# Query copies in halves within the first pass, and maxima rows of twelve heads within the second pass, in a cross-attention layer

## What is computed

```python
q = _split_heads(query_modal @ Wq.T + bq)          # 512 queries, 16 heads of 32
k = _split_heads(key_value_modal @ Wk.T + bk)      # 8192 keys
v = _split_heads(key_value_modal @ Wv.T + bv)
scores = jnp.einsum('bhnd,bhmd->bhnm', q, k) * scale
attn = jax.nn.softmax(scores, axis=-1)
x = jnp.einsum('bhnm,bhmd->bhnd', attn, v)
...
return x @ Wo.T + bo
```

## Time and profile before

| | |
|---|---|
| median of 3 runs | 1815.68 us (1814.56 to 1817.45) |
| profiled execution | 1814.81 us |
| its span | 1813.1 us |
| TensorE (PE) busy | 1572.8 us, 87% |
| VectorE (DVE) busy | 1132.0 us, 62% |
| ScalarE (ACT) busy | 987.8 us, 54% |
| first pass ends, second begins | near 588 to 599 us |
| second pass, first to last score product | 612 to 1194 us |

### The profile page before, as it was taken

The page is one execution under the profiler, slowest core; times in us unless marked ns, Lnnn a source line. Parts: engine busy times, 40 slices in busy tenths (PEclk is TensorE's granted clock), DMA queues, the critical chain, the costliest instruction groups (busy, mean ns, idle before and its releaser), DMA issues. The chain is left out here.

```text
span 1813.1 us, 22494 instructions
## 1 busy us (share of the span) xinstructions
PE 1572.8 (87%) x7524; PEld 774.1 (43%) x7524; DVE 1132.0 (62%) x1774; ACT 987.8 (54%) x1201; POOL 319.6 (18%) x121
## 2 busy tenths in 40 slices
PE   6799999999986699999999999988688006799994
PEld 4566666666653333333333333323343004344442
DVE  5367767767767588898898888864763394100001
ACT  2366666666665588888888888831454101122220
POOL 4755466356430100000000000001000000100001
PEclk9899999999999899999999999999688557799997
DMA  3644445444422944444444444400200850388872
GB/s 139 232 159 178 146 145 186 171 149 162 169 82 69 266 116 117 111 116 116 116 115 112 117 108 118 109 1 0 46 1 1 221 213 2 117 314 313 314 263 82
DMA packets 116884, 249.93 MB, mean 138 GB/s; under 512 B 9401, under 2 KB 25785, under 8 KB 112450
## 3 DMA queue, kind: packets, MB, share of 16 engines
q1 hardware_dynamic: 115088, 244.68, 43.4%
q0 software_dynamic: 1280, 4.20, 0.7%
q10 hardware_dynamic: 434, 0.01, 0.0%
HBM read 182.27 MB, written 61.34 MB: 134 GB/s over the span
## 5 line engine op out<-in xcount | busy, mean ns | idle before, releaser
L692 ACT ACTIVATE att_pr<-att_sc 128x1024 f32<-128x1024 f32 x512 | 496.2, 1022 | 86.3 <-PE att_sc L624 86.2
L464 DVE CUSTOM_DVE_ANT_0 ctx_size<-ctx_tot,ctx_size 128x512 f32<-128x512 f32 x512 | 333.3, 689 | 153.4 <-PE ctx_tot L391 150.4
L722 DVE TENSOR_TENSOR att_tot<-att_tot,att_pr 128x2048 f32<-128x2048 f32 x168 | 385.1, 2292 | 25.2 <-ACT att_pr L692 18.7
L439 ACT ACTIVATE ctx_size<-ctx_dif 128x1024 f32<-128x1024 f32 x256 | 262.2, 1024 | 132.3 <-PE ctx_dif L391 132.3
L624 PE MATMUL att_sc<-g_stacks,att_kst 98*128 98x512 f32 x1024 | 307.5, 422 | 1.6 <-ACT g_stacks L512 1.1
L624 PEld LDWEIGHTS att_sc<-g_stacks,att_kst 98*128 98x128 f32 x1024 | 172.2, 188 | 238.6 <-ACT att_pr L692 211.8
L635 PE MATMUL att_o<-att_pr,att_val 128*32 128x512 f32 x2048 | 272.7, 605 | 0.1
L391 PE MATMUL ctx_dif<-ctx_k_dif,f_q_hi 32*128 32x512 f32 x512 | 129.1, 501 | 26.0 <-ACT ctx_size L439 21.5
L722 DVE TENSOR_TENSOR att_tot<-att_pr 128x2048 f32<-128x2048 f32 x44 | 100.8, 2292 | 59.7 <-ACT att_pr L692 59.7
L391 PE MATMUL ctx_tot<-ctx_k_sum,f_q_hi 32*128 32x512 f32 x512 | 128.4, 499 | 0.0
L1000 POOL MEMSET a_skst<- 2x8192 f32 x1 | 6.9, 6919 | 628.6 <-POOLq L755 628.6
(11 more groups left out here) (243 smaller groups left out, 2093.2 us busy)
## 6 DMA issues: line engine op xcount, KB each, us to landing
m_w<-in_W SPq DMA_DIRECT2D x30, 2048.0 KB, 12.5
att_kst<-keys_scratch SPq DMA_DIRECT2D x192, 256.0 KB, 3.8
f_raw<-in_ctx SPq DMA_DIRECT2D x32, 1024.0 KB, 6.1
keys_scratch<-f_k_hi SPq DMA_DIRECT2D x32, 512.0 KB, 2.8
keys_scratch<-f_k_lo SPq DMA_DIRECT2D x32, 512.0 KB, 3.2
values_scratch<-ctx_v SPq DMA_DIRECT2D x32, 512.0 KB, 3.3
att_val<-values_scratch SPq DMA_DIRECT2D x64, 256.0 KB, 2.7
rows_scratch<-mix_blank SPq DMA_DIRECT2D x1, 3840.0 KB, 26.4
```

What stands on the lines that cost most here:

```text
L439: act.activation(size[:, i % ABS, :], dif[:, :], ACT.Abs).then_inc(s_size, 1)
L464: dve.tensor_tensor_reduce(out=size[:, i % ABS, r * CH:(r + 1) * CH], in0=tot[i % 2][:, r * CH:(r + 1) * CH], in1=size[:, i % ABS, r * CH: ...
L692: act.activation(pr[:, T % RING, 2 * s:2 * s + 2, :], sc[(2 * T + s) % PAIRS][:, :].rearrange("p (j q) -> p j q", j=2), ACT.Exp, scale=SCA ...
L722: dve.tensor_tensor(total[:, :, :], so_far, pr[:, (TILES * g + u) % RING, :, :], ALU.add).then_inc(s_add, 1)
```

## The change

- The order of the three buffer pairs is turned by one, so that item 29 (v 13) is the last to use places 0 to 7 of `stacks` and item 30 (v 14) the last to use places 8 to 15. Behind the value writes of item 29 SyncE copies the queries of heads 0 to 7 (twelve transfers of half the size), behind those of item 30 the queries of heads 8 to 15. Each set waits for `s_out` of the projection before it.
- `maximum_rows` is gone; only heads 0 to 3 are turned in front of the second pass. The four heads of group g+1 are turned in group g, behind the weighted products of its tiles 4, 5, 6 and 7, into the bank `den` (`turn`, at L549 of the changed kernel). Each but the first waits for VectorE's copy of the head before; the first waits for the reciprocal, in groups 1 and 2. VectorE's copy of a head stands behind its addition of the next tile (L718). The first sums of the group wait for the four copies.
- The units of six are replaced by runs of 8, 6 (eight times) and 8 tiles: ten in a group.
- The hardware loops are gone; all 256 tiles are written out.

```diff
+            def queries(half):
+                for place_, part in ((0, f32(c.q_hi[:, :, :])), (1, f32(c.q_hi[:, :, :])), (2, c.q_lo)):
+                    for j in range(HG):
+                        heads = slice(H // 2 * half + j, H // 2 * half + H // 2, HG)
+                        sp.dma_start(f32(c.stacks[HD * place_:HD * place_ + HD, heads, :]),
+                                     part[HD * j:HD * j + HD, 2 * half:2 * half + 2, :]).then_inc(s_stack, 16)
...
-            sp.wait_ge(s_out, 4 * len(ITEMS))
-            for place_, part in ((0, f32(c.q_hi[:, :, :])), (1, f32(c.q_hi[:, :, :])), (2, c.q_lo)):
-                stack_copies(sp, c.stacks, part, place_, s_stack)
+                if at == 3 and o // 4 >= len(ITEMS) - RING and o // 4 < len(ITEMS) - 1:
+
+                    sp.wait_ge(s_out, o + 1)
+                    queries(o // 4 - (len(ITEMS) - RING))
...
-    RING = UNIT = BODY // 2
+    SLOTS = 6
     PAIRS = 3
+    RUNS = (8, 6, 6, 6, 6, 6, 6, 6, 6, 8)
+    TURN = 4
...
+        def turn(pe, out, h):
+            for t in range(NT):
+                i = h * NT + t
+                mm = pe.transpose(out[0:MROW + 2, t * P:(t + 1) * P], shift[:, 2 * i:2 * i + MROW + 2], c.ident[:, :])
+            mm.then_inc(s_turned, 1)
+
+        def turned_at(T):
+            g, u = divmod(T, PER_G)
+            return HG * (g + 1) + u - TURN if g + 1 < G and TURN <= u < TURN + HG else None
...
+            for T in range(TILES):
+                for pair in (2 * T + PAIRS, 2 * T + PAIRS + 1):
+                    if pair < 2 * TILES:
+                        scores(pair)
+                weighted(T)
+                if T - 1 in starts[1:]:
+                    sums(run_of(T) - 1)
+                h = turned_at(T)
+                if h is not None:
+                    if h % HG == 0 and h > HG:
+                        pe.wait_ge(s_rs, h // HG - 1)
+                    if h % HG:
+                        pe.wait_ge(s_row[0], HG // 2 + h - HG)
+                    turn(pe, den, h)
...
+            for T in range(TILES):
+                g, u = divmod(T, PER_G)
+                add(T)
+                h = turned_at(T - 1)
+                if h is not None:
+                    dve.wait_ge(s_turned, h + 1)
+                    dve.tensor_copy(c.stacks[MROW:MROW + 2, h, :], den[MROW:MROW + 2, :]).then_inc(s_row[0], 1)
+                if u == 3 and g:
+                    normalise(g - 1)
...
-            c.hi = [c.stacks[:, 0:DC, :], c.stacks[:, 2 * DC:3 * DC, :], third[:, 0:DC, :]]
-            c.lo = [c.stacks[:, DC:2 * DC, :], c.stacks[:, 3 * DC:4 * DC, :], third[:, DC:2 * DC, :]]
+            c.hi = [c.stacks[:, 2 * DC:3 * DC, :], third[:, 0:DC, :], c.stacks[:, 0:DC, :]]
+            c.lo = [c.stacks[:, 3 * DC:4 * DC, :], third[:, DC:2 * DC, :], c.stacks[:, DC:2 * DC, :]]
```

More of the change, by code:

```diff
@@ L485, in stack_copies @@
             engine.tensor_copy(dst, src).then_inc(s_copy, 1)
[L488 to L525, removed]
@@ L529, in attend_context @@
 def attend_context(nc, c):
     CHUNKS = 3
[L538 to L541, removed]
-    RING = UNIT = BODY // 2
-    PAIRS = 3
[L544 to L550, removed]
+    PER_G = NCH * KT
+    TILES = G * PER_G
+    SLOTS = 6
+    PAIRS = 3
+    RUNS = (8, 6, 6, 6, 6, 6, 6, 6, 6, 8)
+    TURN = 4
+    starts = [g * PER_G + sum(RUNS[:b]) for g in range(G) for b in range(len(RUNS))]
@@ L551, in attend_context, with run_of, adds @@
+    def run_of(T):
+        return max(b for b, s in enumerate(starts) if s <= T)
+    def adds(T):
+        b = run_of(T)
+        return starts[b] - b + max(T - starts[b], 1)
     with ExitStack() as stack:
@@ L571, in attend_context @@
         rows = [sc[i // 2][:, i % 2 * N:i % 2 * N + N] for i in range(4)]
[L572 removed]
+        s_set, s_turned = sem("set"), sem("turned")
+        def turn(pe, out, h):
[6 more added lines that the diff above has]
+            return HG * (g + 1) + u - TURN if g + 1 < G and TURN <= u < TURN + HG else None
         @block.gpsimd
@@ L580, in _ @@
         def _(sp):
[L581 to L586, removed]
+            for m in range(G * NCH):
+                g, chunk, b = m // NCH, m % NCH, m % CHUNKS
+                if m >= CHUNKS:
+                    sp.wait_ge(s_sc, 2 * KT * (m - CHUNKS + 1))
                 for row, part in ((0, 0), (1, 1), (2, 0)):
@@ L599, in _ @@
                     sp.dma_start(c.woT[:, :, :], c.dram["WoT"].rearrange("(k p) o -> p k o", p=P)).then_inc(c.wo_in, 16)
                     load_self_weights(sp, c)
[L601 to L605, removed]
         @block.tensor
         def _(pe):
+            pe.wait_ge(s_set, 4)
+            for h in range(HG):
+                turn(pe, rows[h], h)
@@ L609, in _ @@
             pe.wait_ge(s_ones, CHUNKS)
[L611 to L620, removed]
+            for half in range(2):
+                pe.wait_ge(s_row[half], HG // 2)
@@ L644, in sums @@
                 for j in range(HG):
[L645 to L646 removed]
+                    mm = pe.matmul(den[HD * j:HD * j + HD, :], c.ones[:, :], tot[b % 2][:, j, :],
+                                   start=first, stop=False, skip_group_check=True)
                 mm.then_inc(s_sum, 1)
[L649 to L668 removed]
@@ L679, in _ @@
+            sums(len(starts) - 1)
         @block.scalar
         def _(act):
-            def exponentials(g, i, u):
-                T = TILES * g + u
-                if not isinstance(i, int) or u >= RING:
-                    act.wait_ge(s_pv, T + BODY * i - RING + 1)
-                    act.wait_ge(s_add, ADDS * g + 2 * (UNIT - 1) * i + added(u) - (UNIT - 1))
-                elif g:
-                    act.wait_ge(s_pv, T - RING + 1)
-                    act.wait_ge(s_add, ADDS * (g - 1) + added(TILES + u - RING))
+            for h in range(1, HG, 2):
+                act.wait_ge(s_turned, h + 1)
+                act.activation(c.stacks[MROW:MROW + 2, h, :], rows[h][MROW:MROW + 2, :], ACT.Copy).then_inc(s_row[1], 1)
@@ L710, in add @@
+            for h in range(0, HG, 2):
+                dve.wait_ge(s_turned, h + 1)
+                dve.tensor_copy(c.stacks[MROW:MROW + 2, h, :], rows[h][MROW:MROW + 2, :]).then_inc(s_row[0], 1)
+            def add(T):
+                b = run_of(T)
+                v = T - starts[b]
                 if v == 0:
                     return
-                total = tot[unit % 2]
-                dve.wait_ge(s_exp, 2 * (TILES * g + u + BODY * i) + 2)
+                dve.wait_ge(s_exp, 2 * T + 2)
```

139 lines of the change are left out of this document (60 added, 79 removed).

## The result

The changed kernel takes **1820.09 us** (median of 20 runs, 1815.59 to 1824.63), the kernel before beside it 1816.0 (20 runs, 1813.6 to 1820.62): ratio **1.002**, 95% interval 1.0011 to 1.0029. The profiled execution took 1823.23, with a span of 1821.2 where before had 1813.1.

What follows compares the result with a forecast made beforehand. It took TensorE to set the second pass's pace, with query copies exposed between the passes. Terms summed to +4.9 us: 1819.7 from the profiled 1814.81, 1820.6 from the runs' median; forecast 1820.0, range 1813 to 1825.

Steps and rivals of the forecast that it cites:

- rival A: Second pass: the terms as summed, with the clock falling at TensorE's waits; +3.6 to +9 us, chance 0.55.
- 1 copies: Between the passes: moved query copies are hidden, leaving 0.6 us in place of 10.71; -10.1 us.
- 3 four sums: Second pass: ten sums a group instead of eleven, four fewer at 0.86 us each; -3.4 us.
- part 2: Front of the second pass: twelve heads' rows leave, -5.2 us; first products may still see half clock, +0.4.
- part 5: Second pass: transposes wait for the reciprocal and VectorE's row copies, group 3's first sums for additions; +12.8 us in all.
- part 8: Second pass: TensorE's clock falls after the 3.9 us waits, 1.2 each, and 0.2 for group 0; +2.6 us taken.
- part 6: Runs of 8 at group ends: additions end late, three times 0.55, +1.7 us; at the pass's end +0.8.
- part 4: Within the second pass: turning twelve heads adds work on TensorE, 0.44 us a head; +5.3 us.
- Rival B: Second pass: the clock holds at the waits; +1.9 us, 1816 to 1818.5, no change; chance 0.27.
- Rival C: Second pass: transposes do not wait for VectorE's copy, so the kernel is faster; -4.5 us, 1811; chance 0.12.
- D: Moved copies do not hide, or the third set of keys comes late; up to +5 us on top, 1825; chance 0.03.
- E: Second pass: the removed loops' branches did cost time; up to 3.6 us less, +1.3, 1816; chance 0.03.

Runs made afterwards that it cites:

- e1: The kernel before with the query copies alone moved, second pass unchanged: 1805.89 us, ratio 0.9941 to the kernel before.
- e5: e4 with the sums taken over eight runs of eight tiles in each group: 1797.24 us, ratio 0.9892 to the kernel before.
- e6: e2 with the sums taken over eight runs of eight tiles in each group: 1803.43 us, ratio 0.9912 to the kernel before.
- e2: The changed kernel with all 16 heads turned in front of the second pass again: 1805.49 us, ratio 0.9942 to the kernel before.
- e8: The changed kernel with eleven products of zeros on TensorE ahead of the long wait in groups 1 and 2: 1820.57 us, ratio 1.0018 to the kernel before.
- e13: The changed kernel itself, unaltered, timed once more: 1819.69 us, ratio 1.0022 to the kernel before.
- e10: The changed kernel with runs reordered so that each group ends in a run of four tiles: 1820.76 us, ratio 1.0023 to the kernel before.
- e4: The changed kernel with the twelve row copies within the pass on ScalarE instead of VectorE: 1805.13 us, ratio 0.9937 to the kernel before.
- e3: The changed kernel with VectorE's row copy in front of the next tile's addition instead of behind it: 1813.18 us, ratio 0.9979 to the kernel before.

## Why the prediction was right

Predicted 1820.0, measured 1820.09; rival A, with the mechanism that it named. That the two are 0.1 apart is luck: the interval of the ratio alone is 3 us wide. By parts the traces make +5.9 where the forecast had +4.9 (the rest of the 8.1 between the spans lies outside them), and the medians +4.1. In the table the rows of the groups are the differences shown above, with 0.86 for the sum that went added back, and the slower first tiles (0.77 in group 0) and the change of groups (0.65, 0.64, 0.63) taken out:

| part | predicted | measured |
|---|---|---|
| 1 copies | -10.1 | -10.10; e1 -10.1 |
| 2 front, with the clock | -4.8 | -4.88, and +0.77 in the first four tiles |
| 3 four sums | -3.4 | 0.86 each (e5, e6), -3.4 |
| 4, 5, 8 in group 0 | +4.4 | +3.71 |
| 4, 5, 8 in groups 1, 2 | +8.0 each | +8.00, +7.42 |
| 5 in group 3 | +0.5 | +0.54 |
| 6 changes of groups | +1.7 | +1.91 |
| 6 end of the pass | +0.8 | +1.96 |
| 7 straight-line code | 0 | 2.13 a tile both ways; e2's pass 0.2 under e1's |

Five terms were off, and they mostly cancel.

- *The front* (part 2: -5.2 and +0.4). The agreement of -4.88 is partly luck. With the copies gone and all 16 heads in front, the front takes 15.44 (e1) and 15.41 (e2), 1.1 more than before, as the clock rises later. Against these the twelve heads are worth 6.0, and not 5.2. The forecast took the kernel before as its base.
- *The overlap on VectorE* (part 5, group 0: "2.29 + 0.70 - 0.16 = 2.83 a tile"). It is 3.05. Each row copy starts behind the end of the addition before it and the next addition behind the copy. The overlap had been read from two operations where the second began a new run. The later waits are 0.48, not 0.26. The first wait, on the other hand, was 1.03 and not 1.8, for TensorE itself came 0.7 late out of the half clock at the start.
- *The clock* (part 8, "1.2 each, 2.4"). e8 measures 1.5 for the two groups. The step that the fall also removes later waits was right: in group 1 the last two turns wait for nothing. What varies is how long the half clock lasts, 3.4 or 6.8 (6.8 and 3.4 in the changed kernel, 3.4 and 6.8 in e13, 6.8 twice in e10). The "some 3.4 us of work at half speed" of part 8 had no row behind it: rows 7 show 5.4 us and more at half clock after a wait of 5.2.
- *The end of the pass* (part 6: +0.8). The sums' wait grew by 1.08, and in the profiled execution they ran at half clock, 0.88 more; e13 shows the first without the second. Neither this term nor the 0.55 of the changes of groups was given with a working.
- *The turns* (part 4, "one head per 0.44"). In e4 a turn costs 0.36; the 0.44 was read in front of the pass, where the copies set the pace. Twelve are 1.0 less than part 4 says. The later waits made that up: at full clock (e8) they are 0.49 and 0.48 in group 1, where part 5 has 0.26 each. The first two came as 0.99 and 4.00, forecast as 1.3 and 3.9.

Rival B (the clock holds) is refuted by the windows, and e8 shows what it would have been worth. Rival C fell: VectorE's copy is what the transposes wait for, since moving it one addition forward (e3) gave 7 us by the medians and moving it to ScalarE (e4) 15. D did not come, with the copies issued 28 us early and no wait of TensorE for keys in the second pass. E fell: tiles are 2.12 or 2.13 apart around all sixteen branches of the kernel before, and without any. The Trainium skill, "Runtime: NRT & Kernel Launch", section "Instruction fetch mechanics", has a taken branch out of the pages held cost a fetch. The trace shows no such stall; whether these branches leave the pages held, no run shows.

## What to carry over

Small work that is moved off the front of a stage into its body can be paid by the wait that it brings and not by its own length: twelve turns of 0.36 us and twelve copies of 0.6 to 0.7 cost the pass 19 us, 12 of it the turns' waiting. In groups 1 and 2 the copy stood behind a normalisation and two additions on an engine that was behind already. With the copies on the engine that had just been waiting, the same twelve turns cost 4. Before such a move, read for each handshake which queue has slack at that very tile, and leave an engine's backlog to the middle of a stage, never to its end. A change of several parts is judged by its parts: here -10.1 us was real and hidden by +14.6.

## What the runs showed of the hardware

- An idle time of 4.0 us on TensorE in a dense stream was followed by half clock in all six cases seen (groups 1 and 2 in the changed kernel, e10 and e13). After the one of 2.34 at the pass's end the last sums ran at half clock in two executions of nine (the changed kernel's and e8's), and in a third, e3's, the clock fell within them. Those of 1.60 in e3 were not followed by half clock.
- Transposes alone brought the full clock back. After 17.35 us without work, TensorE did nothing but transposes from 602.57 in the kernel before; the granted clock was 0.50 up to 605.6 and 1.00 from 605.7. In e1 it took 5.5 us.
- The same 1428 matmuls behind the attention took 604.4 us in one trace and 610.9 in another, and 605.2 and 608.9 in two executions of one kernel. For an edit worth 2 us the edited stretch is therefore the better measure, and even that differed by 1.0 between these two executions (620.4 and 621.4).
